# Splitting the E slots of a graph attention layer by whole slots instead of halves

## The chip, the cores and the metric

The kernel runs on one core of one Trainium2 chip. The metric is the device time of one launch in microseconds (us). A core has TensorE (PE, matrix multiplies), VectorE (DVE), ScalarE (ACT), GpSimd (POOL) and the queue engine SyncE (SP). They run separate instruction streams, each in its own order, and meet at semaphores. PE reads its operands from the on-chip memory SBUF and writes to the accumulators PSUM.

## The reference, cut to what matters

Four graph layers run on 8 graphs of 2048 nodes with 128 features. The change touches the second one (layer 1), whose pair scores are additive:

```python
q = feat @ W1.T                        # 2048 x 64
k = feat @ W2.T                        # 2048 x 64
e = relu(q[:, None, :, :] + k[:, :, None, :])      # for every pair (i, j), 64 values
scores = einsum('bijd,d->bij', e, a)
att = softmax(scores + mask, axis=-1)  # mask from adj > 0
return att @ feat
```

Layer 0 is a three-step graph convolution, layer 2 a masked four-head attention and layer 3 a normalised graph product.

## The kernel before, in words

A loop runs over the 8 graphs (batches). In each, layer 1 has 16 tiles of 128 rows. The tensor `e` of one tile would be 128 x 2048 x 64 values. It is made in 16 pieces, called quads. A quad `m` holds four slots of `E`, each 128 partitions x 2048 columns of f32: the partitions carry the 64 features twice, for two neighbouring rows, and the columns are the 2048 values of the other index. One slot is `relu(Q2 + key)`, with the key a scalar for each partition. So four slots make eight rows of scores, and sixteen quads make 128.

`E` has room for three quads (`EQ = 3`, 12 slots); `e_slot` (line 55) turns through them. For each quad

- VectorE (`quad`, line 635) writes slots 0 and 1 whole (lines 639, 640) and the first half of slot 2 (line 641), and then counts up the semaphore `e_dve`;
- ScalarE (`quad`, line 401) writes the second half of slot 2 (line 404) and slot 3 whole (line 405), and then counts up `e_act`;
- TensorE (`quad`, line 930) waits for both counts, multiplies the four slots with a window of the vector `a` in 16 groups (line 940), and counts up `e_used`.

Before they write quad m, VectorE and ScalarE wait until TensorE has used the quad that held its slots: the third before it, or the second before it for quads 8 and 9 of every second tile (`e_lag`, line 60), where the turn of 32 quads through three places starts anew.

The softmax and the product of tile T-1 are done between the quads of tile T, in an order written out by hand. On TensorE (`tile1`, line 956) the 16 transposes of the probabilities (`probs_t1`, line 882 inside `transposes`) stand between quads 6 and 7, and the product with the features (`out1`, line 953) between quads 9 and 10. VectorE (`tile1`, line 680) does the masked minimum (`min1`, line 656) after quad 2, the copies of the last two quarters of the transposed probabilities out of PSUM (`evac1`, line 667) after quad 7, the final scaling (`finish1`, lines 673 and 677) after quad 11, and the mask of the tile itself (line 648) after quad 14. ScalarE (`tile1`, line 419) does the exponential (line 409) after quad 4, its two copies (line 342, `evac1`) after quad 7, and the row sums of the adjacency (line 390) after quad 12. Both copy a tile's keys (`keys`) before its quad 0. The first tile of each batch has no tile before it, so it has none of this work but the mask and the row sums. Its quad 0 opens the layer. Tiles 0 and 1 are written out, and tiles 2 to 15 are a loop of seven turns with two tiles in each; the engines loop separately.

The copies at line 667 wait for `pt1_ps`, which TensorE counts up after every fourth transpose.

Of the kernel before, what the change touches and what calls it, by code (L numbers as in the profile page):

```python
# [7 lines left out]
ALU = mybir.AluOpType  # L8
ACT = mybir.ActivationFunctionType

P = 128
NB, N, D = 8, 2048, 128
# [42 lines left out]
def e_slot(u, m):  # L55

    return 4 * ((u * QUADS + m - TURN) % (2 * QUADS) % EQ)


def e_lag(u, m):  # L60

    return 2 if u * QUADS + m - TURN in (0, 1) else EQ
# [16 lines left out]
def build(nc, x, adj, Ws, bs, gammas, betas, W1, W2, a_vec, Wq, bq, Wk, bk, Wv, bv, Wo, bo, Bw, out):  # L79
# [4 lines left out]
    with ExitStack() as ctx:  # L84
        def sb(name, shape, dt=F32, where=None):
            return (where or ctx).enter_context(nc.sbuf_tensor(name, shape, dt))

        def sem(name):
            return ctx.enter_context(nc.semaphore(name))
# [38 lines left out]
        kd = sb("kd", [P, 2, 64])  # L128
        ka = sb("ka", [P, 2, 64])
# [14 lines left out]
        with ExitStack() as ph:  # L144
            E = sb("E", [P, 4 * EQ, N], where=ph)
            Q2 = sb("Q2", [P, N], where=ph)
# [47 lines left out]
        e_dve = sem("e_dve")  # L194
# [145 lines left out]
        def _(act):  # L340
# [59 lines left out]
            def quad(T, m, u, first):  # L400
                if not (first and m < EQ):
                    act.wait_ge(e_used, T * QUADS + (m - e_lag(u, m) + 1))
                s = e_slot(u, m)
                nc.scalar.activation(E[:, s + 2, N // 2:N], Q2[:, N // 2:N], ACT.Relu, bias=ka[:, u, 32 + m:33 + m])  # L404
                nc.scalar.activation(E[:, s + 3, :], Q2[:, :], ACT.Relu, bias=ka[:, u, 48 + m:49 + m]).then_inc(e_act, 1)  # L405

            def exp1(T, u):
# [11 lines left out]
            def tile1(b, t, u, tail, half, first):  # L419
                T = b * NT + t  # L420
                keys(t, T, u, first)
                for m in range(QUADS):
                    quad(T, m, u, not tail)
                    if tail and m == 4:
                        exp1(T - 1, 1 - u)
                    if tail and m == 7:
                        evac1(T - 1, 1 - u)
                    if m == 12:
                        degrees(b, t, T, half, u, tail)
# [33 lines left out]
            with act.Fori(0, NB) as b:  # L463
# [29 lines left out]
                for c in range(NC):  # L493
                    act.wait_ge(qk2_ps, b * 8 + 4 + c + 1)
                    nc.scalar.activation(AGG[:, c * CH:(c + 1) * CH], ps[:, c, :], ACT.Identity,
                                         bias=bk_c[:, 0:1]).then_inc(qk2_act, 1)
# [33 lines left out]
        def _(dve):  # L530
# [69 lines left out]
            def biased(b, l, c, Z, HB):  # L600

                dve.wait_ge(zn_rdy, (b * HEV + l) * NC + c + 1)
                row = b0[:, l, :].rearrange("p (o d) -> p o d", o=1).broadcast_to([P, TPC, D])
                return nc.vector.scalar_tensor_tensor(out=chunk(HB, c), in0=chunk(Z, c), scalar=0.0, in1=row,
                                                      op0=ALU.max, op1=ALU.add)
# [29 lines left out]
            def quad(T, m, u, first):  # L635
                if not (first and m < EQ):
                    dve.wait_ge(e_used, T * QUADS + (m - e_lag(u, m) + 1))
                s = e_slot(u, m)
                nc.vector.tensor_scalar(E[:, s, :], Q2[:, :], kd[:, u, m:m + 1], 0.0, ALU.add, ALU.max)  # L639
                nc.vector.tensor_scalar(E[:, s + 1, :], Q2[:, :], kd[:, u, 16 + m:17 + m], 0.0, ALU.add, ALU.max)  # L640
                nc.vector.tensor_scalar(E[:, s + 2, 0:N // 2], Q2[:, 0:N // 2], kd[:, u, 32 + m:33 + m], 0.0,  # L641
                                        ALU.add, ALU.max).then_inc(e_dve, 1)

            def mask1_tile(b, T, half, u):

# [34 lines left out]
            def tile1(b, t, u, tail, half, first):  # L680

                T = b * NT + t
                keys(t, T, u, first)
                for m in range(QUADS):
                    quad(T, m, u, not tail)
                    if tail and m == 2:
                        min1(T - 1, 1 - u)
                    if tail and m == 7:
                        evac1(T - 1, 1 - u)
                    if tail and m == 11:  # L690
                        finish1(t - 1, T - 1, 1 - u)
                    if m == 14:
                        mask1_tile(b, T, half, u)
# [79 lines left out]
            with dve.Fori(0, NB) as b:  # L773
# [8 lines left out]
                for c in range(NC):  # L782
                    last = biased(b, 0, c, Z, HB)
# [63 lines left out]
                for half in range(2):  # L847
                    for g in (2 * half, 2 * half + 1):
                        dve.wait_ge(x3_ps, b * NC + g + 1)
                        xg = X[:, g * TPC:(g + 1) * TPC, :]  # L850
                        last = nc.vector.tensor_tensor(xg, ps[:, 4 + g, :].rearrange("p (t d) -> p t d", d=D), xg,
                                                       ALU.add)
# [290 lines left out]
```

## Time and profile before

| what | value |
|---|---|
| median of three runs | 13545.26 us (13543.89 to 13548.91) |
| the profiled execution, its own time | 13528.44 us |
| its span, first to last instruction | 13526.8 us |
| TensorE busy | 12596.1 us, 93% of the span |
| VectorE busy | 10002.4 us, 74% |
| ScalarE busy | 9186.4 us, 68% |
| mean granted TensorE clock | 0.968 of full |

The profile is one execution of the program. Its groups give, for each source line, an engine and an operation, the number of instructions, their busy time and mean duration, and then the time that the engine stood idle just before them with what ended it. The durations of neighbouring instructions on one engine can overlap a little, so the starts in a timeline give the pace and the durations give the end.

### The profile page before, as it was taken

What the parts mean: (1) busy time and instruction counts of PE and PEld (TensorE: products, weight loads), DVE (VectorE), ACT (ScalarE), POOL (GpSimd) and SP (SyncE); (2) the same over time, 40 slices, a digit from 0 to 9 for tenths busy, and PEclk for the clock granted to TensorE, in tenths of its full rate; (3) what the DMA queues carried; (4) which work ended last, traced back from release to release, by engine and by line L of the source; (5) the groups of instructions that cost most, each with busy time, mean ns of one, the idle gap of its engine ahead of it and who ended that gap; (6) DMA issues with size and microseconds to landing.
All of it is one profiled execution on the core that took longest, in us unless ns stands there. A gap on an engine that the chain in (4) does not pass through costs nothing.

```text
span 13526.8 us, 272613 instructions
## 1 busy us (share of the span) xinstructions
PE 12596.1 (93%) x110721; PEld 6210.2 (46%) x110721; DVE 10002.4 (74%) x13927; ACT 9186.4 (68%) x8920; POOL 349.3 (3%) x505
## 2 busy tenths in 40 slices
PE   8998989989899898998989989899898998989989
PEld 3333833338333383333833338333383334833348
DVE  4887658876588765887658876588765887658876
ACT  3886638866388663886638866388663886638866
POOL 0000000000000000000000000000000000000000
PEclk9999999999999999999999999999999999999999
DMA  1001300013000130001300013000130001300012
GB/s 67 17 20 45 122 32 17 20 45 126 27 17 20 48 124 26 18 19 46 125 27 17 20 45 126 28 17 20 48 127 23 20 17 48 128 22 20 17 48 87
DMA packets 124332, 636.17 MB, mean 47 GB/s; under 512 B 15120, under 2 KB 49680, under 8 KB 49680
## 3 DMA queue, kind: packets, MB, share of 16 engines
q1 hardware_dynamic: 92688, 420.78, 8.8%
q0 software_dynamic: 18432, 134.23, 2.5%
q10 hardware_dynamic: 12288, 67.13, 2.3%
q8 instruction: 790, 12.94, 0.4%
q14 instruction: 134, 1.10, 0.0%
HBM read 546.57 MB, written 8.39 MB: 41 GB/s over the span
## 4 chain that ended last, share of the span: by engine, by line
PE 72%; issue 15%; DVE 8%; ACTq 2%; POOL 1%; DMA 1%; ACT 1%; DVEq 0%; POOLq 0%; SPq 0%
PE ps L940 45%; PE ps L982 8%; PE ps L995 4%; PE ps L953 4%; PE ps L973 3%; PE ps L1112 3%; DVE E L640 3%; ACTq L502 2%; DVE E L639 2%; PE ps L882 2%; DVE E L641 2%; PE ps L1100 1%; POOL rstd L319 1%; DMA adj_ring<-in_adj 1%; PE ps L1004 1%
## 5 line engine op out<-in xcount | busy, mean ns | idle before, releaser
L940 PE MATMUL ps<-E,a_win 128*32 128x512 f32 x65536 | 7139.8, 594 | 152.3 <-DVE E L641 87.9
L940 PEld LDWEIGHTS ps<-E,a_win 128*32 128x32 f32 x65536 | 2115.5, 110 | 4997.0 <-issue 4739.6
L405 ACT ACTIVATE E<-Q,ka 128x2048 f32<-128x2048 f32 x2048 | 4078.7, 1992 | 0.0
L404 ACT ACTIVATE E<-Q,ka 128x1024 f32<-128x1024 f32 x2048 | 2347.4, 1146 | 620.8 <-PE ps L940 618.7
L639 DVE TENSOR_SCALAR E<-Q,kd 128x2048 f32<-128x2048 f32 x2048 | 2628.3, 1283 | 143.7 <-PE ps L940 97.1
L640 DVE TENSOR_SCALAR E<-Q,kd 128x2048 f32<-128x2048 f32 x2048 | 2624.7, 1282 | 0.0
L924 PE MATMUL ps<-adj_res,H 128*128 128x512 f32 x3072 | 1354.9, 599 | 198.3 <-ACT H L347 198.3
L641 DVE TENSOR_SCALAR E<-Q,kd 128x1024 f32<-128x1024 f32 x2048 | 1533.4, 749 | 0.0
L342 ACT ACTIVATE PT<-ps 128x512 f32<-128x512 f32 x1792 | 1001.5, 596 | 750.8 <-PE ps L882 475.8
L708 DVE CUSTOM_DVE_ANT_0 T<-ps,adj_ring 128x2048 f32<-128x2048 f32 x512 | 1173.4, 2292 | 256.6 <-PE ps L973 209.1
L433 ACT ACTIVATE T<-T,nmin 128x2048 f32<-128x2048 f32 x512 | 1022.0, 1996 | 306.8 <-issue 306.0
L982 PE MATMUL ps<-ident,T 128*128 128x128 f32 x8192 | 1132.6, 282 | 21.8 <-ACT T L433 11.7
L342 ACT ACTIVATE AGG<-ps 128x512 f32<-128x512 f32 x224 | 127.7, 596 | 1380.2 <-PE ps L924 1233.4
L924 PEld LDWEIGHTS ps<-adj_res,H 128*128 128x128 f32 x3072 | 583.7, 193 | 901.1 <-issue 701.2
L982 PEld LDWEIGHTS ps<-ident,T 128*128 128x128 f32 x8192 | 888.2, 142 | 233.1 <-issue 203.6
L973 PE MATMUL ps<-kst,qcur 128*128 128x512 f32 x2048 | 624.5, 427 | 239.4 <-DMA kst<-kl 236.5
L610 DVE TENSOR_TENSOR HT<-ps,HW 128x512 f32<-128x512 f32 x96 | 66.1, 689 | 886.6 <-PE ps L915 886.6
L995 PE MATMUL ps<-PT,V 128*32 128x128 f32 x16384 | 658.9, 279 | 0.0
L667 DVE COPY PT<-ps 128x512 f32<-128x512 f32 x256 | 165.7, 687 | 611.8 <-PE ps L882 611.8
L953 PEld LDWEIGHTS ps<-H,PT 128*128 128x128 f32 x4096 | 470.2, 193 | 110.6 <-issue 110.6
L953 PE MATMUL ps<-H,PT 128*128 128x128 f32 x4096 | 494.4, 279 | 7.0 <-DVE PT L667 7.0
L973 PEld LDWEIGHTS ps<-kst,qcur 128*128 128x128 f32 x2048 | 359.3, 196 | 302.3 <-DMA kst<-kl 193.9
(109 smaller groups left out, 7443.8 us busy)
## 6 DMA issues: line engine op xcount, KB each, us to landing
adj_ring<-in_adj SPq DMA_DIRECT2D x384, 1024.0 KB, 4.8
adj_res<-in_adj POOLq DMA_DIRECT2D x128, 1024.0 KB, 6.9
qst<-qh ACTq DMA_DIRECT2D x64, 256.0 KB, 5.0
qst<-ql ACTq DMA_DIRECT2D x64, 256.0 KB, 5.0
kst<-kh ACTq DMA_DIRECT2D x64, 256.0 KB, 5.0
kst<-kl ACTq DMA_DIRECT2D x64, 256.0 KB, 5.0
X<-in_x SPq DMA_DIRECT2D x128, 64.0 KB, 2.0
out_x<-HW SPq DMA_DIRECT2D x8, 1024.0 KB, 10.0
```

The source lines that it names most:

```text
L404: nc.scalar.activation(E[:, s + 2, N // 2:N], Q2[:, N // 2:N], ACT.Relu, bias=ka[:, u, 32 + m:33 + m])
L405: nc.scalar.activation(E[:, s + 3, :], Q2[:, :], ACT.Relu, bias=ka[:, u, 48 + m:49 + m]).then_inc(e_act, 1)
L639: nc.vector.tensor_scalar(E[:, s, :], Q2[:, :], kd[:, u, m:m + 1], 0.0, ALU.add, ALU.max)
L640: nc.vector.tensor_scalar(E[:, s + 1, :], Q2[:, :], kd[:, u, 16 + m:17 + m], 0.0, ALU.add, ALU.max)
L641: nc.vector.tensor_scalar(E[:, s + 2, 0:N // 2], Q2[:, 0:N // 2], kd[:, u, 32 + m:33 + m], 0.0, ALU.add, ALU.max).then_inc(e_dve, 1)
L708: nc.vector.tensor_tensor_reduce(out=T2[:, h, :], in0=ps[:, 0:4, :].rearrange("p c n -> p (c n)"), in1=ring[:, u, :], scale=1.0, scalar=BI ...
L924: last = mm(ps[:, c, :], H[:, t, :], A[:, t, c * CH:(c + 1) * CH], start=(t == 0), stop=(t == NT - 1))
L940: last = mm(ps[QROWS * grp:QROWS * (grp + 1), 4 * u + c, :], win, E[:, s + grp, c * CH:(c + 1) * CH], start=(m == 0), stop=(m == QUADS - 1 ...
L953: last = mm(ps[:, 4 * u, 0:D], PT1[:, j * P:(j + 1) * P], H[:, j, :], start=(j == 0), stop=(j == NT - 1))
L973: last = mm(ps[:, c, :], qcur[:, u, h, :], kst[:, h, c * CH:(c + 1) * CH], start=True, stop=True)
L982: last = nc.tensor.transpose(ps[:, 4 + g % 2, k * P:(k + 1) * P], T2[:, h, j * P:(j + 1) * P], ident[:, :])
L995: last = mm(ps[HD * k:HD * (k + 1), 6 + h % 2, 0:P], V[:, g * TPC + k, h * HD:(h + 1) * HD], PT2[:, g, k * P:(k + 1) * P], start=(g == 0), ...
```

## The change: whole slots, in turn

Slot 2 is no longer shared. In even quads VectorE writes slots 0, 1 and 2 and ScalarE writes slot 3. In odd quads VectorE writes slots 0 and 1, and ScalarE writes slots 2 and 3. The count of `e_dve` and `e_act` stays one for each quad, on the last instruction. TensorE's stream and all other work stay as they were.

```diff
@@ ScalarE, quad
                 s = e_slot(u, m)
-                nc.scalar.activation(E[:, s + 2, N // 2:N], Q2[:, N // 2:N], ACT.Relu, bias=ka[:, u, 32 + m:33 + m])
+                if m % 2:
+                    nc.scalar.activation(E[:, s + 2, :], Q2[:, :], ACT.Relu, bias=ka[:, u, 32 + m:33 + m])
                 nc.scalar.activation(E[:, s + 3, :], Q2[:, :], ACT.Relu, bias=ka[:, u, 48 + m:49 + m]).then_inc(e_act, 1)
@@ VectorE, quad
                 nc.vector.tensor_scalar(E[:, s, :], Q2[:, :], kd[:, u, m:m + 1], 0.0, ALU.add, ALU.max)
-                nc.vector.tensor_scalar(E[:, s + 1, :], Q2[:, :], kd[:, u, 16 + m:17 + m], 0.0, ALU.add, ALU.max)
-                nc.vector.tensor_scalar(E[:, s + 2, 0:N // 2], Q2[:, 0:N // 2], kd[:, u, 32 + m:33 + m], 0.0,
-                                        ALU.add, ALU.max).then_inc(e_dve, 1)
+                last = nc.vector.tensor_scalar(E[:, s + 1, :], Q2[:, :], kd[:, u, 16 + m:17 + m], 0.0, ALU.add, ALU.max)
+                if m % 2 == 0:
+                    last = nc.vector.tensor_scalar(E[:, s + 2, :], Q2[:, :], kd[:, u, 32 + m:33 + m], 0.0,
+                                                   ALU.add, ALU.max)
+                last.then_inc(e_dve, 1)
```

## Rows read from the trace of the kernel before

**Rows 1.** The page's busy line: engine, busy us, share, instructions.

```profile
PE 12596.1 (93%) x110721; PEld 6210.2 (46%) x110721; DVE 10002.4 (74%) x13927; ACT 9186.4 (68%) x8920; POOL 349.3 (3%) x505
```

**Rows 2.** Groups of the page: line, engine, operation, count; busy, mean ns; idle before.

```profile
L940 PE MATMUL ps<-E,a_win 128*32 128x512 f32 x65536 | 7139.8, 594 | 152.3 <-DVE E L641 87.9
...
L405 ACT ACTIVATE E<-Q,ka 128x2048 f32<-128x2048 f32 x2048 | 4078.7, 1992 | 0.0
L404 ACT ACTIVATE E<-Q,ka 128x1024 f32<-128x1024 f32 x2048 | 2347.4, 1146 | 620.8 <-PE ps L940 618.7
L639 DVE TENSOR_SCALAR E<-Q,kd 128x2048 f32<-128x2048 f32 x2048 | 2628.3, 1283 | 143.7 <-PE ps L940 97.1
L640 DVE TENSOR_SCALAR E<-Q,kd 128x2048 f32<-128x2048 f32 x2048 | 2624.7, 1282 | 0.0
...
L641 DVE TENSOR_SCALAR E<-Q,kd 128x1024 f32<-128x1024 f32 x2048 | 1533.4, 749 | 0.0
```

**Rows 3.** Waits of PE, whole trace: us in total, times, longest.

```profile
PE ps L940 <- DVE E L641: 87.9, 131, 4.2
PE ps L940 <- issue: 64.4, 45, 1.7
```

**Rows 4.** One stretch in layer 1: us, busy of each engine, PEclk, DMA share, GB/s.

```profile
340.00:1220.00 880.00, 865.42 (x7924) 310.21 (x7920) 770.73 (x793) 751.87 (x553) 0.00 (x0) 1.00 0.05 18
```

**Rows 5.** Timeline of PE, two tiles: start us, us, line [idle before <-releaser].

```profile
2424.74 24.24 PE L940 MATMUL ps<-E,a_win 128*32 128x512 f32 x224 [1.25 <-issue]
2448.91 1.97 PE L882 MATMUL ps<-ident,T 128*128 128x128 f32 x16
2450.81 3.64 PE L940 MATMUL ps<-E,a_win 128*32 128x512 f32 x32
2454.88 7.07 PE L940 MATMUL ps<-E,a_win 128*32 128x512 f32 x64 [0.43 <-DVE E L641]
...
2465.65 44.84 PE L940 MATMUL ps<-E,a_win 128*32 128x512 f32 x416
...
2516.38 7.07 PE L940 MATMUL ps<-E,a_win 128*32 128x512 f32 x64 [0.42 <-DVE E L641]
```

**Rows 6.** Timeline of DVE: around quad 8 and around quad 3.

```profile
2450.48 1.29 DVE L667 COPY PT<-ps 128x512 f32<-128x512 f32 x2 [5.16 <-PE ps L882]
2451.68 1.28 DVE L639 TENSOR_SCALAR E<-Q,kd 128x2048 f32<-128x2048 f32 x1
2452.88 1.28 DVE L640 TENSOR_SCALAR E<-Q,kd 128x2048 f32<-128x2048 f32 x1
2454.07 0.75 DVE L641 TENSOR_SCALAR E<-Q,kd 128x1024 f32<-128x1024 f32 x1
2454.74 1.28 DVE L639 TENSOR_SCALAR E<-Q,kd 128x2048 f32<-128x2048 f32 x1
...
2486.53 1.29 DVE L639 TENSOR_SCALAR E<-Q,kd 128x2048 f32<-128x2048 f32 x1
...
2492.11 1.29 DVE L639 TENSOR_SCALAR E<-Q,kd 128x2048 f32<-128x2048 f32 x1 [0.23 <-DVE nmin L656]
...
2494.50 0.75 DVE L641 TENSOR_SCALAR E<-Q,kd 128x1024 f32<-128x1024 f32 x1
```

**Rows 7.** Timeline of ACT: quads 8 and 9 of a tile where quad 9 waits.

```profile
2512.08 1.15 ACT L404 ACTIVATE E<-Q,ka 128x1024 f32<-128x1024 f32 x1
...
2516.03 1.15 ACT L404 ACTIVATE E<-Q,ka 128x1024 f32<-128x1024 f32 x1 [0.90 <-PE ps L940]
2517.08 1.99 ACT L405 ACTIVATE E<-Q,ka 128x2048 f32<-128x2048 f32 x1
2518.98 1.14 ACT L404 ACTIVATE E<-Q,ka 128x1024 f32<-128x1024 f32 x1
```

**Rows 8.** Timeline of the opening of the layer in the first batch.

```profile
247.98 0.75 DVE L641 TENSOR_SCALAR E<-Q,kd 128x1024 f32<-128x1024 f32 x1
...
248.82 13.70 PE L940 MATMUL ps<-E,a_win 128*32 128x512 f32 x100 [4.15 <-DVE E L641]
```

## The prediction

> **What bounds the kernel now.** I read the page's busy line first: TensorE is busy 93% of the span, VectorE 74%, ScalarE 68% [rows 1]. A share over four unlike layers doesn't say what one stage waits for, so the groups came next. The scores of layer 1 are the largest: 65,536 matmuls with 7139.8 us busy, and only 152.3 us idle before them [rows 2]. In a stretch that lies wholly inside this stage, TensorE is busy 865.42 us of 880, VectorE 770.73, ScalarE 751.87, and the granted clock is 1.00, so the upper level, 2.4 GHz [rows 4]. So TensorE sets the pace here, and the two writers wait for it: 618.7 of ScalarE's 620.8 us and two thirds of VectorE's 143.7 us of idle time ahead of a quad end with a matmul [rows 2]. A change to the writers can be worth no more than TensorE's idle time, or cost what it adds to it. The view of waits divides that: 87.9 us in 131 waits end with VectorE's line 641, and 64.4 us in 45 are "issue" [rows 3].
>
> The timeline of TensorE shows where the 131 are. The same gap of 0.43 us stands before quad 8 of each tile that has a tail, after the transposes and quad 7 [rows 5]. That is 15 tiles in 8 batches, 120 x 0.43 = 51.6 us. The opening of a batch has one of 4.15 [rows 8], 8 x 4.15 = 33.2. Three of 1.1 us remain (120 + 8 + 3 = 131; 51.6 + 33.2 + 3.1 = 87.9). Those three and the 45 of "issue" are one thing, the turn of TensorE's own loop, six in a batch, of which one shows as 1.25 us [rows 5].
>
> Why quad 8 waits can be followed on VectorE [rows 6]. It stands idle 5.16 us until TensorE's transposes are far enough, then copies (2450.48), writes the three pieces of quad 8 from 2451.68, and the last of them, started at 2454.07, ends at 2454.82. TensorE goes on at 2454.88, 0.06 later. TensorE was through with quad 7 0.43 us before. This chain, transposes, copies, quad 8's write, is the one place in a tile where the end of a write is on the path.
>
> **The change part by part.** *VectorE, even quads.* The half slot of 749 ns becomes a whole one of 1282, the mean of the same operation on line 640 [rows 2]. The end of the quad comes 1282 - 749 = 533 ns later. The trace has no third whole slot in a row, but the same operation with this shape twice in each quad. Durations and starts can be mixed for the two ends of this cost: pace of a whole slot less duration of a half, 1.20 - 0.75 = 0.45 us, and duration of a whole one less pace of a half, 1.28 - 0.67 = 0.61 us [rows 6]. I take 533 ns, duration against duration, since the last write's end is what TensorE waits for.
>
> Quad 8 is even in every tile (the parity is m's alone). Its write starts at the same 2451.68, as what it waits for, the transposes, isn't changed, and ends at 2455.35. The gap becomes 0.43 + 0.53 = 0.96 us. In 120 tiles: 120 x 0.533 = 64.0 us, all on the path.
>
> *The opening of a batch.* Quad 0 is even too. TensorE waits for the write that ends at 247.98 + 0.75 = 248.73 and starts at 248.82 [rows 8]. Nothing covers this one: 8 x 0.533 = 4.3 us. The next quads still come in time. VectorE would end quad 1 at about 251.7, where TensorE wants it at about 252.8.
>
> *The other even quads* (2, 4, 6, 10, 12, 14, and 0 in later tiles). VectorE's pace is 1.20 us from start to start for a whole slot and 0.67 for a half; a quad took 3.06 (2451.68 to 2454.74) [rows 6]. Now an even one takes 3.59 and an odd one 2.39. TensorE takes 24.17 / 7 = 3.45 a quad [rows 5]. An even quad alone is longer than this, but three quads fit into E, so a write may start two quads of TensorE (6.9 us) before its reader. It needs only that the lead isn't used up. The lead is smallest behind the minimum of line 656. Before, quad 3 is ready at 2494.50 + 0.75 = 2495.25, and TensorE, with 9 quads from 2465.65, wants it at 2496.7: 1.4 us early. After: quad 2 still starts at 2486.53, when TensorE frees its slots, and ends 0.53 later; the minimum and quad 3 shift by this, and quad 3, now odd, is shorter by 0.67. It is ready at 2495.1, 1.6 early. Quad 4 is even: 2495.0 + 2.39 + 1.28 = 2498.7 against 2500.1. Quads 5 and 6 have 2 us and more. So these cost nothing. The cover is 1.4 us, and if it were gone, each tile would pay the lack.
>
> *ScalarE.* A quad took 1.05 + 1.90 = 2.95 us from start to start [rows 7]; now 1.90 in even and 3.80 in odd quads. Quad 8 gets shorter and isn't the last to arrive. Quad 9 is the one to watch in every second tile, since there its slots come free only with quad 7 (start at 2516.03, after a wait of 0.90) [rows 7]. After: 2516.03 + 1.90 + 1.99 = 2519.92. TensorE's quad 8 starts at 2516.38 + 0.53 = 2516.91 and takes 3.45, so it wants quad 9 at 2520.36. ScalarE is 0.4 us early, and only because quad 8 is later by itself. I put this at nothing. Behind the exponential (line 409) quad 5 has about 2 us.
>
> *What is saved.* A tile's writes take VectorE 16 x 3.06 = 49.0 us before and 8 x (3.59 + 2.39) = 47.8 after, ScalarE 47.2 and 45.6. Each does 1024 instructions less. Both wait for TensorE, so this adds to their idle time: VectorE's 5.16 us ahead of the copies becomes longer [rows 6].
>
> On this the Trainium skill says two things, in Perfetto Trace Analysis, section Optimizing Scalar/DVE Operations. Larger operations can raise throughput where the engine is saturated, and where it isn't but makes bubbles on another engine, breaking instructions up may let work be done sooner. The trace has the second case, and the change goes the other way, so by that sentence it loses. By the first one there would be a gain, which is the second rival below.
>
> **The sum.** 64.0 + 4.3 = 68.3 us. The profiled execution has 13528.44 us, 1.6 beside its span of 13526.8, and would have 13597. The median of the runs is 13545.26, 17 us over the profiled one (0.12%, which nothing here explains). Against it the forecast is 13613.6, so 13613, 0.50% slower. What a measurement of this kernel tells from no change is about 0.2%, 27 us.
>
> **The rivals.**
> *1. ScalarE late at quad 9.* The margin of 0.4 us is worked out from durations of one stretch. If it is off by as much again, 64 tiles pay up to 0.4 us more, 26 us, and the time is 13639. For it speaks that this is the thinnest margin. Against it: ScalarE's whole slot takes 1992 ns in the mean of 2048 and 1.99 in this very place [rows 2, 7]. Chance 0.06.
>
> *2. The writers' throughput is what counts.* If VectorE's and ScalarE's savings of 1.2 and 1.6 us a tile reached quad 8's write, the gap of 0.43 would be gone: 120 x 0.43 = 51.6 us gained, 13494, faster. It decides from the point where quad 8's write starts 0.53 us earlier than now (no loss), and at 0.96 all is gained. Against it: the start hangs on TensorE's transposes, for which VectorE waits 5.16 us [rows 6]. Chance 0.02.
>
> *3. The turns of the loop get shorter.* The 48 turns hold 64.4 + 3.1 = 67.5 us [rows 3]. If the smaller programs of the two writers took that away, the sum would be about nil, 13546. It decides at 1.4 us a turn; a third of it leaves 13591. Against it: TensorE's own instructions and its branch are the same, and both writers are quads ahead there. The Trainium skill, Runtime: NRT & Kernel Launch, section Instruction fetch mechanics, says that a taken branch to a target outside the pages at hand makes the engine fetch first. That is a matter of each engine's own stream, and no row here shows another's part in it. Chance 0.03.
>
> *4. The lead isn't there.* If an even quad's excess over TensorE's pace were paid each time, 3.59 - 3.45 = 0.14 us x 8 x 128 = 143 us, some 13756 with the rest. It needs a ring of two quads in effect. The start at 2486.53 for a quad wanted at about 2493.2 shows the lead whole [rows 5, 6]. Chance 0.03.
>
> A longer gap could also bring the clock down. But TensorE already stands still for up to 1.7 us at the turns of the loop, and the clock is 1.00 over seven of these tile pairs [rows 3, 4]. 0.96 us is less.
>
> **How the numbers follow.** The forecast has 0.86, and in it the term's bounds (0.45 to 0.61 us, 128 times) give 58 to 78 us, so 13603 to 13623; the scatter between executions (5 us in three runs, 17 to the profiled one) comes on top. The range 13583 to 13640 takes in the first rival and the milder form of the third, and leaves out the rest. Faster (rival 2, and little for what I don't see) 0.03, the same 0.04 (rival 3), slower 0.93.
>
> **What would show it.** In the profile after, TensorE's gap before quad 8 is 0.96 us rather than 0.43, and ended by VectorE; the waits of line 940 for VectorE's quads add up to about 87.9 + 68 = 156 us. VectorE's write of quad 8 starts 1.2 us after the copies as now. No new gap stands at quad 9 or behind the minimum. "issue" stays near 64 us. Busy time of VectorE and ScalarE falls, and that of TensorE stays. The prediction is wrong if the gap at quad 8 keeps its size, if a second one stands in the tile, or if the waits grow as said and the time doesn't.

## The result, and the profile after

The changed kernel takes 13624.97 us in the median of six runs (13616.61 to 13639.23), the kernel before 13544.58 (13516.75 to 13556.91) beside it. The ratio is 1.006, with a 95% interval from 1.005 to 1.007: 80 us slower, where 68 were forecast. The median lies inside the forecast range of 13583 to 13640 us and 12 us over its centre of 13613. The profiled execution took 13630.98 us with a span of 13629.3.

The groups of the page, as in [rows 2]. Line 940 is now 943, 639 and 640 are 640 and 641, VectorE's third slot is line 643, and ScalarE's slots are lines 405 (odd quads) and 406.

```profile
PE 12631.3 (93%) x110721; PEld 6217.9 (46%) x110721; DVE 9855.4 (72%) x12903; ACT 8980.6 (66%) x7896; POOL 354.2 (3%) x505
...
L943 PE MATMUL ps<-E,a_win 128*32 128x512 f32 x65536 | 7137.9, 594 | 222.7 <-DVE E L643 152.4
...
L406 ACT ACTIVATE E<-Q,ka 128x2048 f32<-128x2048 f32 x2048 | 4001.9, 1991 | 14.0
L640 DVE TENSOR_SCALAR E<-Q,kd 128x2048 f32<-128x2048 f32 x2048 | 2626.1, 1282 | 210.8 <-PE ps L943 165.1
...
L405 ACT ACTIVATE E<-Q,ka 128x2048 f32<-128x2048 f32 x1024 | 2054.9, 2007 | 856.2 <-PE ps L943 856.2
...
L643 DVE TENSOR_SCALAR E<-Q,kd 128x2048 f32<-128x2048 f32 x1024 | 1311.7, 1281 | 0.0
```

VectorE has 147 us less to do than in [rows 1] and ScalarE 206, and yet the kernel is slower. The matmuls of line 943 take as long as in [rows 2], and their idle time is up by 70.4 us. The waits of TensorE answer to [rows 3]:

```profile
PE ps L943 <- DVE E L643: 152.4, 128, 4.6
...
PE ps L943 <- ACT E L406: 46.2, 33, 1.5
...
PE ps L943 <- issue: 24.2, 15, 1.8
```

The first row is 120 x 0.96 + 8 x 4.64 = 152.3. The forecast had about 156 here; three turns of the loop that stood in this row before (3.1 us) are no longer in it. The other two rows are the 48 turns (33 + 15). They sum to 46.2 + 24.2 = 70.4 us, 67.5 before. That ScalarE is named in 33 of them is presumably the profile's choice of the last to arrive, as the gaps keep their size. The timeline of TensorE answers to [rows 5]; the starts differ, since the whole layer is later:

```profile
2470.74 1.97 PE L885 MATMUL ps<-ident,T 128*128 128x128 f32 x16
2472.63 3.64 PE L943 MATMUL ps<-E,a_win 128*32 128x512 f32 x32
2477.23 7.07 PE L943 MATMUL ps<-E,a_win 128*32 128x512 f32 x64 [0.96 <-DVE E L643]
2484.24 3.84 PE L956 MATMUL ps<-H,PT 128*128 128x128 f32 x32
2488.01 44.84 PE L943 MATMUL ps<-E,a_win 128*32 128x512 f32 x416
```

The only gap listed in the tile is still the one ahead of quad 8, and 0.43 us have become 0.96. On VectorE the chain is the one of [rows 6] with a longer last link; its wait ahead of the copies has grown from 5.16 to 5.66 us:

```profile
2472.30 1.29 DVE L670 COPY PT<-ps 128x512 f32<-128x512 f32 x2 [5.66 <-PE ps L885]
2473.51 1.28 DVE L640 TENSOR_SCALAR E<-Q,kd 128x2048 f32<-128x2048 f32 x1
2474.70 1.28 DVE L641 TENSOR_SCALAR E<-Q,kd 128x2048 f32<-128x2048 f32 x1
2475.90 1.28 DVE L643 TENSOR_SCALAR E<-Q,kd 128x2048 f32<-128x2048 f32 x1
```

The write of line 643 ends at 2477.18, and TensorE goes on at 2477.23. (2477.18 less 2473.51 is 3.67; it was 3.14 in [rows 6].)

**Where the rest is.** The profiled pair differs by 102.5 us, and the gaps explain 70. I cut both traces at three points of each batch: the first matmul of a score in layer 1, the end of the last one, and the first score of layer 2. Layer 1 takes 7922.0 us in eight batches before and 7986.6 after (+64.6). The stretch behind it takes 514.0 and 538.7 (+24.7). Busy time and granted clock of this stretch in the first batch, before and after:

```profile
1239.19:1302.20 63.01, 23.09 (x113) 15.95 (x113) 25.93 (x65) 13.36 (x20) 3.75 (x4) 0.73 0.46 104
```

```profile
1247.72:1315.18 67.46, 28.55 (x112) 19.64 (x112) 26.01 (x65) 13.48 (x20) 3.75 (x4) 0.65 0.43 97
```

The work is the same, some 113 matmuls; VectorE and ScalarE take the same time for it. TensorE takes 5.5 us more, at a mean clock of 0.65 and not 0.73. (This pair is one of the widest; over eight batches the stretches differ by 3.1 us in the mean.) The largest single piece is the 32 matmuls of the last tile's product. They took 3.81 us before, at a granted clock of 1.00 (2.4 GHz), and here 6.05 at a mean of 0.61, so mostly at the lower level (1.2 GHz):

```profile
1248.15 3.81 PE L953 MATMUL ps<-H,PT 128*128 128x128 f32 x32 [0.88 <-DVE PT L667]
```

```profile
1257.01 6.05 PE L956 MATMUL ps<-H,PT 128*128 128x128 f32 x32 [0.88 <-DVE PT L670]
```

In both kernels TensorE has stood still for 4.74 us ahead of the transposes that feed this product, waiting for the last exponential. The prediction said that TensorE's busy time would stay. It rose by 35.2 us (12596.1 to 12631.3), and 28.2 of these lie in the eight stretches behind layer 1.

### The profile page after: what moved, and what is told of

The parts are those of the page before. It is cut to its first block, busy times and chain, and to the rows that moved or that the text cites. A ratio compares the mean times of both kernels' runs of the same rounds, so it can differ in the third digit from the quotient of the medians.

```text
span 13629.3 us, 270565 instructions
## 1 busy us (share of the span) xinstructions
PE 12631.3 (93%) x110721; PEld 6217.9 (46%) x110721; DVE 9855.4 (72%) x12903; ACT 8980.6 (66%) x7896; POOL 354.2 (3%) x505
## 4 chain that ended last, share of the span: by engine, by line
PE 75%; issue 13%; DVE 5%; ACTq 2%; ACT 2%; POOL 1%; DMA 1%; DVEq 0%; POOLq 0%; SPq 0%
PE ps L943 48%; PE ps L985 8%; PE ps L998 4%; PE ps L956 4%; PE ps L976 3%; PE ps L1115 3%; ACTq L503 2%; PE ps L885 2%; PE ps L1103 1%; POOL rstd L319 1%; DVE E L640 1%; DVE E L643 1%; DVE E L641 1%; ACT E L405 1%; ACT E L406 1%
## 5 line engine op out<-in xcount | busy, mean ns | idle before, releaser
L406 ACT ACTIVATE E<-Q,ka 128x2048 f32<-128x2048 f32 x2048 | 4001.9, 1991 | 14.0
L640 DVE TENSOR_SCALAR E<-Q,kd 128x2048 f32<-128x2048 f32 x2048 | 2626.1, 1282 | 210.8 <-PE ps L943 165.1
L641 DVE TENSOR_SCALAR E<-Q,kd 128x2048 f32<-128x2048 f32 x2048 | 2623.9, 1281 | 0.0
L405 ACT ACTIVATE E<-Q,ka 128x2048 f32<-128x2048 f32 x1024 | 2054.9, 2007 | 856.2 <-PE ps L943 856.2
L643 DVE TENSOR_SCALAR E<-Q,kd 128x2048 f32<-128x2048 f32 x1024 | 1311.7, 1281 | 0.0
```

Of the source, the lines that this page charges most:

```text
L405: nc.scalar.activation(E[:, s + 2, :], Q2[:, :], ACT.Relu, bias=ka[:, u, 32 + m:33 + m])
L641: last = nc.vector.tensor_scalar(E[:, s + 1, :], Q2[:, :], kd[:, u, 16 + m:17 + m], 0.0, ALU.add, ALU.max)
L643: last = nc.vector.tensor_scalar(E[:, s + 2, :], Q2[:, :], kd[:, u, 32 + m:33 + m], 0.0, ALU.add, ALU.max)
```

## The experiments

Ten more runs were made: eight edited kernels, and each of the two kernels once more. Theory P is the prediction's: the end of VectorE's write of quad 8 is on the path, and the change costs what it adds there. Its rival T says that the load of the two writers is what counts, and A that each even quad pays a little. For each run the layer and the stretch behind it were cut as above.

**One part alone.** `e1_q8_alone` and the kernels up to `e3` share this form of the split; `dve_cols` gives the columns of slot 2 that VectorE writes:

```diff
-                nc.scalar.activation(E[:, s + 2, N // 2:N], ...)
+                cut = dve_cols(u, m)
+                if cut < N:
+                    nc.scalar.activation(E[:, s + 2, cut:N], ...)
...
-                nc.vector.tensor_scalar(E[:, s + 2, 0:N // 2], ...).then_inc(e_dve, 1)
+                if cut:
+                    last = nc.vector.tensor_scalar(E[:, s + 2, 0:cut], ...)
+                last.then_inc(e_dve, 1)
```

```diff
+def dve_cols(u, m):
+    return N if m == 8 else N // 2
```

> One part alone: only quad 8 of each tile has three whole slots on VectorE and one on ScalarE, all other quads stay halved. Theory P (the end of VectorE's write of quad 8 is the path): TensorE's gap before quad 8 goes from 0.43 to 0.96 us in 120 tiles, the opening keeps its 4.15 us, no gap at quad 9; 0.533 x 120 = 64 us slower than before, about 13609. Theory T (what counts is how much the writers have to do): one quad in sixteen is changed, so a sixteenth of the loss, some 5 us, about 13550. Theory A (each even quad pays a little): an eighth of 80 us, 10 us.

Measured: 13614.83 us against 13537.11, ratio 1.0057 (1.0043 to 1.0071), 78 us slower, where P had 64. The gap is 0.96 us; the row below is 120 of these, the eight openings of 4.15 and one turn of the loop:

```profile
PE ps L950 <- DVE E L650: 149.7, 129, 4.2
```

Layer 1 is 64.9 us longer than in the first profile of the kernel before, as P says; the rest lies in the stretch behind it (table below). One quad of sixteen, changed alone, makes a loss as large as that of the whole change. T and A fall.

**The same part undone.**

```diff
+def dve_cols(u, m):
+    return N // 2 if m == 8 else N if m % 2 == 0 else 0
```

> The change with one part undone: quad 8 is halved as before, all other quads are split by whole slots in turn. Theory P: the gap before quad 8 is back at 0.43 us; the opening costs 0.53 x 8 = 4 us more; ScalarE's two whole slots of quad 9 end at 2516.03 + 3.89 = 2519.92 against 2519.83 where TensorE wants them, so a new gap of about 0.15 us in 64 tiles, 10 us; in all 14 us slower than before, about 13559. Theory T: 15/16 of the loss stays, 75 us, about 13620. Theory A: 7/8 of it, 70 us.

Measured: 13571.57 us, ratio 1.0027 (1.0015 to 1.0038), 34 us slower; P had said 14. The gap before quad 8 is back at 0.43 us:

```profile
458.86 2.01 ACT L411 ACTIVATE E<-Q,ka 128x2048 f32<-128x2048 f32 x1 [0.90 <-PE ps L950]
...
459.22 7.33 PE L950 MATMUL ps<-E,a_win 128*32 128x512 f32 x64 [0.43 <-DVE E L650]
...
460.77 3.88 ACT L412 ACTIVATE E<-Q,ka 128x2048 f32<-128x2048 f32 x2
```

ScalarE's second slot of quad 9 ends at 460.77 + 1.99 = 462.76, and quads 8 and 9 take 7.33 us in place of 7.07. So the lateness at quad 9 is 0.26 us, not 0.15, and the profile lists no gap for it. Most of the difference is the time from the end of ScalarE's write to TensorE's start: in the waits that ScalarE ends it is 0.145 us (see `e3`), where the 0.15 had been worked out with the 0.06 that VectorE's writes show. Layer 1 is 14.0 us longer in all, the openings add 4, and the stretch behind the layer 13 more than in the kernels before (below). That is 31. The losses of `e1` and `e2` (78 and 34 us) don't add up to that of the change (80), since quad 9 is late only where quad 8 isn't.

**Less on VectorE at quad 8.**

```diff
+def dve_cols(u, m):
+    return 0 if m == 8 else N // 2
```

> Quad 8 alone with two whole slots on each of the two engines, all else halved as before. Theory P: VectorE is done with quad 8 at 2454.16, ScalarE at 2450.57 + 1.90 + 1.99 = 2454.46, TensorE is free at 2454.45; the gap shrinks from 0.43 to about 0.07 us and is now ended by ScalarE; 0.36 x 120 = 43 us faster than before, about 13502. Theory T: ScalarE has 0.95 us more to do in a tile and VectorE 0.67 less; no change or slightly slower.

Measured: 13506.64 us, ratio 0.9975 (0.9964 to 0.9987), 30 us faster. P had 43. ScalarE now ends the wait, as expected, but 0.17 us late rather than 0.07. In all 120 places TensorE starts 0.144 to 0.146 us after the end of ScalarE's write; after VectorE's write it was 0.055 us [rows 6], and that had been taken for both:

```profile
PE ps L950 <- ACT E L412: 19.9, 120, 0.2
```

Layer 1 is 27.5 us shorter, close to 120 x 0.26 = 31. In this pair a kernel with less on VectorE and more on ScalarE is faster, and one with less on both, the change, is slower: it is the place that counts.

**The chain cut at its start.** In `tile1` of VectorE:

```diff
-                    if tail and m == 7:
+                    if tail and m == 8:
                         evac1(T - 1, 1 - u)
```

> The kernel before with one step moved: VectorE copies the last two quarters of the transposed probabilities out of PSUM after it has written quad 8, not ahead of it; all quads halved as before. Theory P with its cause (the write of quad 8 hangs behind the copies, which hang on the transposes): quad 8 is ready 2 us early, the gap before it is gone, and quad 9 is ready at 2516.0 + 3.14 = 2519.2 against 2519.4, so 0.43 x 120 = 52 us faster, about 13493. If the copies are wanted early by someone else (the product after quad 9), a gap appears before that product and the gain is less or nil.

Measured: 13476.24 us, ratio 0.9954 (0.9941 to 0.9968), 61 us faster, the fastest of all (52 were expected). No gap is listed in the tile any more. VectorE writes quad 8 in the time in which it used to wait for the transposes, and copies after it:

```profile
452.57 1.29 DVE L639 TENSOR_SCALAR E<-Q,kd 128x2048 f32<-128x2048 f32 x1 [3.10 <-PE ps L940]
453.77 1.28 DVE L640 TENSOR_SCALAR E<-Q,kd 128x2048 f32<-128x2048 f32 x1
454.97 0.74 DVE L641 TENSOR_SCALAR E<-Q,kd 128x1024 f32<-128x1024 f32 x1
455.63 1.28 DVE L667 COPY PT<-ps 128x512 f32<-128x512 f32 x2
```

```profile
452.43 1.97 PE L882 MATMUL ps<-ident,T 128*128 128x128 f32 x16
454.33 10.55 PE L940 MATMUL ps<-E,a_win 128*32 128x512 f32 x96
464.81 3.84 PE L953 MATMUL ps<-H,PT 128*128 128x128 f32 x32
```

The product follows quad 9 without a gap, so nobody had wanted the copies earlier. Layer 1 lost 72.7 us, more than the 51.6 that the gaps held. Quad 7, cut off by a gap, is listed with 3.64 us, and the next quad starts 4.07 us after it [rows 5]; without the gap a quad takes 3.44. So each gap of 0.43 us had cost 0.63 (120 x 0.63 = 76). The listed gap leaves out the 0.2 us by which the records of quad 7 reach past its pace. The same holds for 0.96, so the growth of 0.53 is not touched by this. Whether those 0.2 us are real work of the last matmuls or come from the way the profile models their ends, no run here tells.

**The change and the moved copies together.** The diff of `e4`, applied to the changed kernel.

> The changed kernel with the one step of e4: VectorE copies the last two quarters of the transposed probabilities after it has written quad 8. Theory P: the gap of 0.96 us before quad 8 goes (120 x 0.96 = 115 us). But then TensorE is at quad 8 earlier, and in every second tile ScalarE's two whole slots of quad 9, which can't start before quad 7 is used, are 0.55 us late: 64 x 0.55 = 35 us. So 80 us less than the changed kernel, within 10 us of the kernel before. The cost of whole slots has then moved to quad 9. If the writers' load were what counts, it would be as fast as e4 or faster, since both engines have less to do than there.

Measured: 13542.46 us against 13547.29 of the kernel before, ratio 0.9996 (0.9987 to 1.0005), so no change from before, and 86 us off the changed kernel run beside it (`e7`). The cost of whole slots has moved to quad 9, as expected: the gap there is 0.68 us in every second tile, and ScalarE ends it. That the expected 80 us came out is partly luck. In layer 1 the removed gap was worth 137.3 us and not 115 (7986.6 less the 7849.3 of `e4`), and quad 9 costs 53.7 and not 35 (7903.0 less 7849.3); the two errors cancel.

```profile
457.45 2.01 ACT L405 ACTIVATE E<-Q,ka 128x2048 f32<-128x2048 f32 x1 [1.94 <-PE ps L943]
459.36 3.88 ACT L406 ACTIVATE E<-Q,ka 128x2048 f32<-128x2048 f32 x2
```

```profile
453.74 7.07 PE L943 MATMUL ps<-E,a_win 128*32 128x512 f32 x64
461.49 3.64 PE L943 MATMUL ps<-E,a_win 128*32 128x512 f32 x32 [0.68 <-ACT E L406]
```

Against `e4` it has less work on both engines, and it is 56 us slower (each taken against its own runs of the kernel before).

**The turn the other way round.**

```diff
+def dve_cols(u, m):
+    return N if m % 2 else 0
```

> The change with its turn the other way round: VectorE and ScalarE write two and two whole slots in even quads, three and one in odd. The writers' load in a tile is that of the changed kernel. Theory P: quad 8 is even, so its gap is that of e3 (0.17 us in place of 0.43, -31 us); quad 9 has three slots on VectorE, about 0.3 us late in every second tile (+19); in the opening ScalarE's two slots end 0.8 us later than before (+6). About 6 us faster than before, 13531, and 85 us faster than the change. Theory T: as the change, 13617.

Measured: 13542.86 us, ratio 1.0001 (0.9992 to 1.001), the same as before and 85 us under the change (`e7`), with the same load. The 6 us that P expected over the kernel before are too few to be told from nothing here. Layer 1 is 19.0 us shorter than before; the openings (5.0 us each) and the stretch behind the layer take that back. At quad 9 VectorE's third slot is late by some 0.2 us in every second tile (quads 8 and 9 take 7.28 us in place of 7.07), again without a listed gap.

**The changed kernel again.** No edit.

> The changed kernel once more, on the chip and beside the runs of the kernel before that the other experiments share. Its gaps in layer 1 must come out as in its first profile (0.96 us, 120 times, and 4.6 at eight openings). What is open is the rest, 12 us in the medians and 34 in the profiled pair: it lies between the end of layer 1 and the start of the next one, where the granted clock falls. If this rest belongs to the changed length of layer 1, the stretch from the end of layer 1 to the first scores of layer 2 takes 67 us again, against 63 to 66 before; if it is chance of one execution, it takes 63 to 66 here.

Measured: 13628.04 us, ratio 1.0056 (1.0043 to 1.007). Layer 1 takes 7986.6 us, to the tenth what it took in the first profile, and the stretch behind it 535.5 (538.7 there). The sum of the eight isn't chance of one execution, though single stretches scatter (64.8 to 67.6 us).

**The cost made larger.**

```diff
# ScalarE, in quad 8: the second half of slot 3 alone
# VectorE, in quad 8: slot 2 whole, and
+                    nc.vector.tensor_scalar(E[:, s + 3, 0:N // 2], Q2[:, 0:N // 2], kd[:, u, 48 + m:49 + m], 0.0,
+                                            ALU.add, ALU.max).then_inc(e_dve, 1)
```

> The suspected cost made larger: in quad 8 alone VectorE writes three and a half slots and ScalarE half a one; all else halved as before. Theory P: VectorE's write ends 1.20 us later than before, the gap goes from 0.43 to 1.63 us, 144 us slower, about 13681. A cost that saturates, or one that ScalarE's lighter load gives back, would show as less.

Measured: 13705.78 us, ratio 1.0115 (1.01 to 1.0131), 158 us slower. The gap is 1.62 us, layer 1 is 145.0 us longer (144 expected), and most of the rest lies behind the layer. The cost grows in proportion.

```profile
PE ps L949 <- DVE E L647: 194.9, 120, 1.6
```

**Is the clock's part the kernel's own?** Two more, one without an edit and one that only swaps ScalarE's two writes.

> The kernel before once more, with a profile, to learn how much the stretch from the end of layer 1 to the first scores of layer 2 differs between executions of one program. In its first profile eight such stretches took 62.9 to 66.0 us, 514 in all, at a granted clock of 0.69 to 0.73; in the two of the changed kernel 64.8 to 67.5, 539 and 536, at 0.65 to 0.72. If the clock's part belongs to the kernel, this one gives 514 to 520 again. If it is chance of an execution, it can be anything from 505 to 540. The time itself: no change, 13545.

> The kernel before with ScalarE's two writes of a quad in the other order (the whole slot first, then the half); layer 1 keeps its length of 990.2 us a batch to a tenth, as both ends of a quad stay within 0.05 us and ScalarE isn't last at quad 8. If the clock's part goes by the length of layer 1 (the theory that is left for the 10 to 25 us that the gaps don't explain), the stretch behind it takes about 64 us a batch, 514 in all, as in the kernel before, and the time is unchanged. If it goes by other details of the writers' programs, it may take 67.

```diff
-                nc.scalar.activation(E[:, s + 2, N // 2:N], ...)
                 nc.scalar.activation(E[:, s + 3, :], ...)
+                nc.scalar.activation(E[:, s + 2, N // 2:N], ...).then_inc(e_act, 1)
```

Measured: 13544.83 and 13545.29 us against 13543.45, both ratios 1.0 (0.9991 to 1.001). The stretches behind layer 1 take 519.7 and 521.2 us in all, where 514 to 520 and 514 were expected. So three profiles of unchanged pace give 514 to 521, and two of the changed kernel 536 and 539.

Here is the account of all kernels, in us. Layer 1 is taken against 7924 and the stretch behind it against 518, the means of the kernel before's two profiles and of the three. "Sum" adds 8 times what the opening grew by (the opening isn't in layer 1's length).

```
                    layer 1          behind it      openings    sum   measured
changed kernel      7986.6  +62.5    537.1  +18.8    +3.9       +85    +80
e1 quad 8 alone     7986.9  +62.8    535.4  +17.1     0         +80    +78
e2 quad 8 halved    7936.0  +11.9    531.4  +13.1    +3.9       +29    +34
e3 two and two      7894.5  -29.6    519.2   +0.9     0         -29    -30
e4 copies later     7849.3  -74.8    529.5  +11.2     0         -64    -61
e5 change and e4    7903.0  -21.1    535.2  +16.9    +3.9        -0     -5
e6 other way round  7903.0  -21.1    536.9  +18.6    +6.8        +4     -4
e8 quad 8 heavy     8067.0 +142.9    528.2   +9.9     0        +153   +158
```

"Measured" is the difference of the medians. No line is off by more than 9 us. The remainder of a batch, layers 2, 3 and 0, scatters between profiles by some 20 us in all (4426 to 4447 for seven), and by 18 in the three profiles of unchanged pace alone (4426 to 4444).

## Why the prediction was right

*What bounds the kernel.* TensorE did set the pace, and the 131 waits divided as said. `e4`, which takes away the chain from copies to quad 8, removes all 120 gaps and no others. The price of 51.6 us for these gaps was low: removing them gave 72.7 in layer 1. The forecast needed only their growth, so this didn't hurt it.

*Quad 8.* The added 0.533 us were sized from a whole and a half slot's duration. The gap grew by 0.53 (64 us in 120 tiles, and layer 1 grew by 62.5 to 64.6), and `e1` shows that this quad alone carries the loss. The dose in `e8`, 1.20 us more, gave 1.19.

*The opening.* 4.3 us were forecast; the gap went from 4.15 to 4.64, 3.9 us. The reading of [rows 8] had a small error. ScalarE's slot of quad 0 ended at 246.69 + 1.99 = 248.68, and TensorE's start at 248.82 is the 0.145 us behind it that `e3` shows; all eight openings have this distance. VectorE's write, ended at 248.73, would with its 0.055 have let TensorE start at 248.79. So ScalarE ended this wait before, though the profile names VectorE, and the growth is smaller than 0.533:

```profile
246.69 1.99 ACT L405 ACTIVATE E<-Q,ka 128x2048 f32<-128x2048 f32 x1
```

*The other even quads.* Taken at nothing, and no gap appeared there. The stretch of [rows 4] has a clock of 1.00 in the changed kernel too.

*ScalarE at quad 9.* The margin of 0.4 us between the end of the write and TensorE's start was forecast and is there: ScalarE is done at 2540.29 + 1.99 = 2542.28 in the tile whose quad 9 starts at about 2542.7.

```profile
2540.29 3.89 ACT L406 ACTIVATE E<-Q,ka 128x2048 f32<-128x2048 f32 x2
```

Of these 0.4 us the release takes 0.145, which the prediction left out, so about 0.3 were to spare. The margin held only because quad 8 was late. Where quad 8 comes earlier, in `e2` and `e5`, ScalarE is late at quad 9. This was the first rival, which was dormant in the change and real beside it.

*The writers' throughput,* the second rival, gave nothing, although VectorE and ScalarE were relieved of 147 and 206 us. *The turns of the loop,* the third, kept their 67 to 73 us in each profile. *The lead,* the fourth, held: behind the minimum of the next tile VectorE is done with quad 3 at 2517.48, and TensorE wants it at 2488.01 + 9 x 3.44 = 2519.0, 1.5 us later; 1.6 were forecast.

*What the sum left out.* It has 68 us, and layer 1 with its openings has 62.5 + 3.9 against the mean of two profiles of the kernel before. The stretch behind the layer added 19, at a lower mean clock. The prediction asked about the clock only inside layer 1 and not at its end, and so put this term at nothing. It is more than the 12 us between forecast and median. That the median came out no higher is within the scatter of the layers that weren't cut out here, and not something that the prediction knew.

*Still open:* why the clock falls earlier behind layer 1. In 15 of the 16 stretches of the changed kernel's two profiles it falls to 1.2 GHz 3.0 to 3.9 us after the last score, and the last tile's product then takes 5.7 to 6.1 us. In the 24 stretches of the three profiles of unchanged pace it falls 4.1 to 5.4 us after the last score (once 2.2), and the product takes 3.81 us in 22 of them. This product makes up 14.7 of the 18.8 us. The cause isn't the whole slots: `e4` has halves everywhere and a slow product in four batches of eight, and `e1` and `e8`, with halves everywhere but in quad 8, have it in six and four. It isn't just a longer layer either: `e4` is shorter. Kernels with equal lengths of layer 1 have nearly equal stretches behind it (7986.6 and 7986.9: 535 to 539; 7903.0 twice: 535 and 537; 7922 to 7926 three times: 514 to 521), which speaks for the moment at which the layer ends. But single batches of one program scatter with nearly the same length of layer 1 (62.8 to 66.0 us in the first profile of the kernel before, 64.6 to 69.0 in `e1`), and no run here sets that moment by itself, so this is argued, not shown.

## What to carry to other kernels

Where an engine is busy three quarters of the time and waits for another, as VectorE here, its total work need not be what it costs; look for the one place in the cycle where its end releases the bounding engine, and size an edit by what it does to that instruction. A wait in an in-order queue holds what stands behind it. Here two copies that nobody needed yet stood ahead of a write that everyone waited for, and moving one line (`e4`) gained more than any split of the slots that was tried. Before a split is made coarser, find its margin at each place where the buffer is short, and expect that curing one gap uncovers the next.

## What the runs showed of the hardware

A small gap in TensorE's records understates its cost by about 0.2 us in this stage: gaps listed with 0.43 us were worth about 0.6 when removed (72.7 us over 120), and a lateness of 0.26 us wasn't listed at all but showed as two quads of 7.33 us in place of 7.07.

TensorE starts 0.055 us after the end of the VectorE write that it waits for (120 places in the kernel before, in the changed one and in `e8`), and 0.145 us after the end of a ScalarE write (120 places in `e3`, 64 in `e5`, and the eight openings of the kernel before). In these openings VectorE's write ended 0.05 us later than ScalarE's, and still it was ScalarE's that TensorE followed.

The same stretch of a program, with the same instructions, took 63 us where the mean granted clock in it was 0.73 and 67.5 where it was 0.65. Between the kernel before and the changed one, which differ only in the layer ahead, it moved by 19 us in eight batches, a quarter of the effect that was to be measured.
